# A Mamba-style scan kernel: norm and output stages reordered, both directions summed on TensorE, scan states in SBUF

## The reference

```
x = x + conv(layernorm_over_channels(x))       # conv: norm over the 64x64 pixels, weight, bias,
                                               # dt = softplus(xn . dt_w + dt_b),
                                               # out[t] = exp(dt*A) * out[t-1] + xn[t], t over 1024 channels
t = tokens(x)                                  # 4096 tokens x 1024
xz = (layernorm(t) @ in_proj_w.T).T            # 2 x 2048 channels x 4096 tokens
x, z = split(xz)
y  = direction(x) + reverse(direction(reverse(x)))    # forward and backward weights differ
out = t + nan_to_num((y * silu(z)) @ out_proj_w.T)

direction(x):  xc = conv1d(x) + b ; [dt, B, C] = xc @ xproj_w.T
               u = clip(xc); delta = softplus(clip(dt @ dtproj_w.T + b) + b)
               h[n] = exp(delta * A[n]) * h[n] + (delta * u) * B[n]     # 16 states n, over tokens
               y = sum over n of C[n] * h[n]  +  u * D
```

## Time and profile before

| what | us |
|---|---|
| median of 3 runs | 8618.31 (8612.55 to 8621.57) |
| the profiled execution | 8615.87 |
| its span, first to last instruction | 8614.1 |
| TensorE busy | 7207.2 (84%) |
| VectorE busy | 7548.3 (88%) |
| ScalarE busy | 4928.4 (57%) |
| GpSimd busy | 6814.0 (79%) |

### The profile page before, as it was taken

How to read it: one execution, slowest core, us unless ns; L and a number is a source line. 1 busy time by engine, 2 the same in 40 slices (tenths; PEclk the granted TensorE clock), 3 DMA queues, 4 the chain that set the end, 5 groups by cost and what they waited for, 6 DMA issues and landing times. The chain is left out here.

```text
span 8614.1 us, 107712 instructions
## 1 busy us (share of the span) xinstructions
PE 7207.2 (84%) x28624; PEld 4128.4 (48%) x28624; DVE 7548.3 (88%) x8364; ACT 4928.4 (57%) x11720; POOL 6814.0 (79%) x3026
## 2 busy tenths in 40 slices
PE   7449888888888888876788888888888887769999
PEld 4243455455545555544455545455555555534444
DVE  7940999999999999999999999999999999934443
ACT  2552666666666666666666666666666666610000
POOL 1310999999999999999999999999999999921110
PEclk9679999999999999987899999999999998879999
DMA  3263231313131313121223232323232322154442
GB/s 83 58 188 129 73 112 64 113 65 114 64 113 67 113 64 113 66 100 42 98 73 124 74 126 72 124 76 124 72 124 78 122 73 104 47 175 137 137 138 81
DMA packets 540787, 843.35 MB, mean 98 GB/s; under 512 B 112576, under 2 KB 260032, under 8 KB 522816
## 3 DMA queue, kind: packets, MB, share of 16 engines
q1 hardware_dynamic: 540224, 837.03, 29.4%
HBM read 583.83 MB, written 253.02 MB: 97 GB/s over the span
## 5 line engine op out<-in xcount | busy, mean ns | idle before, releaser
L1114 POOL TENSOR_TENSOR scan_w<-scan_du,scan_bcast_b 128x2048 f32<-128x2048 f32 x1023 | 4629.4, 4537 | 3.6 <-DMA scan_bcast_b<-bc 3.6
L1163 DVE TENSOR_TENSOR_SCAN scan_h<-scan_da,scan_state,scan_w 128x512 f32<-128x512 f32 x3072 | 3787.0, 1282 | 21.8 <-issue 14.5
L920 PE MATMUL scan_yT<-all_ident,scan_hc 128*128 128x128 f32 x12288 | 1992.4, 300 | 1010.9 <-DVE scan_hc L1173 995.5
L1020 ACT ACTIVATE scan_da<-scan_delta,scan_prm 128x512 f32<-128x512 f32 x4096 | 2803.6, 685 | 0.0
L920 PEld LDWEIGHTS scan_yT<-all_ident,scan_hc 128*128 128x128 f32 x12288 | 1466.6, 151 | 1974.6 <-DVE scan_hc L1173 1741.8
L1173 DVE TENSOR_TENSOR scan_hc<-scan_h,scan_bcast_c 128x512 f32<-128x512 f32 x3072 | 1955.5, 682 | 16.9 <-ACT scan_state L1000 16.9
L812 PE MATMUL scan_in_ps<-scan_hn,scan_win 128*128 128x512 f32 x3840 | 1741.0, 596 | 13.3 <-issue 13.3
L1000 ACT ACTIVATE scan_state<-scan_h 128x1 f32<-128x1 f32 x3072 | 518.6, 169 | 1770.7 <-DVE scan_h L1163 1768.8
L1123 POOL TENSOR_TENSOR scan_hp<-scan_hs,scan_bcast_c 128x512 f32<-128x512 f32 x1024 | 1306.5, 1276 | 73.7 <-issue 47.0
L1163 DVE TENSOR_TENSOR_SCAN scan_hs<-scan_da,scan_state,scan_w 128x512 f32<-128x512 f32 x1024 | 1297.5, 1267 | 32.1 <-ACT scan_da L1020 31.9
L812 PEld LDWEIGHTS scan_in_ps<-scan_hn,scan_win 128*128 128x128 f32 x3840 | 697.0, 192 | 723.2 <-issue 723.2
(11 more groups left out here) (128 smaller groups left out, 5547.8 us busy)
## 6 DMA issues: line engine op xcount, KB each, us to landing
yT<-scan_y_out SPq DMA_DIRECT2D x257, 256.0 KB, 2.0
scan_win<-winx SPq DMA_DIRECT2D x128, 512.0 KB, 3.5
xc<-scan_xc_out SPq DMA_DIRECT2D x256, 256.0 KB, 2.0
scan_xc<-xc SPq DMA_DIRECT2D x256, 256.0 KB, 3.6
scan_bcast_b<-bc SPq DMA_DIRECT2D x64, 1024.0 KB, 7.8
scan_bcast_c<-bc SPq DMA_DIRECT2D x64, 1024.0 KB, 7.8
scan_win<-winz SPq DMA_DIRECT2D x128, 512.0 KB, 4.6
scan_x<-x_pad SPq DMA_DIRECT2D x128, 257.5 KB, 2.6
```

The costliest lines, as they stand in the source:

```text
L920: last = nc.tensor.matmul(yT[:, tb], hc[:, i % NOUT, tb * P:(tb + 1) * P], ident[:], is_transpose=True, start=(i == 0 and tb == 0), stop=( ...
L1020: nc.scalar.activation(da[:, n % 2], delta[:, s], ACT.Exp, scale=decay(b, n)).then_inc(S["exp_done"], 1)
L1114: nc.gpsimd.tensor_tensor(w[:, g], du[:, s].unsqueeze(1).to_broadcast([P, G, T]), bcast_b[:, g * G:(g + 1) * G], ALU.mult).then_inc(S["w_d ...
L1163: nc.vector.tensor_tensor_scan(flip(b, h_slot(n)), flip(b, da[:, n % 2]), flip(b, w[:, n // G, n % G]), state_of(b, n), ALU.mult, ALU.add) ...
```

## The change

- Norm (n3): `affine` moves to ScalarE, `add_log` to GpSimd, where it alternates with the scalings, two tiles ahead. ScalarE loads one table set at the start.
- Scan: h moves from PSUM to SBUF. The two banks are y_ps and early_ps. TensorE's new `sum_y(b)`, for forward units, transposes the unit's y_out and the stored y of the backward unit of the same tokens and channels (loaded to y_back by SP) into y_ps: 8 transposes. ScalarE's `y_copy` moves it to y_sum, and SP stores it in y by channels. Only the backward units' sums go to yT now. z_out has one slot instead of two. The zero matmuls around a projection go: its first and last matmul open and close it. TensorE's loop over `before_scan` is written out.
- Out: y and z are loaded, in four slots; no sum on GpSimd, no transposes; VectorE multiplies y and silu(z), both in SBUF. wout is loaded after the first chunk's y and z, and each projection waits for its own tile.

The core of the diff:

```
 stage_channel_scan
+            def scale(j):
+                for s in range(2):
+                    nc.gpsimd.tensor_tensor(xn[...], xn[...], rstd2[:], ALU.mult).then_inc(scaled, 1)
+            def add_log(j):                                     # GpSimd
+                for s in range(2):
+                    pool.wait_ge(relu_done, j * 2 + s + 1)
+                    pool.wait_ge(log_done, j * 2 + s + 1)
+                    nc.gpsimd.tensor_tensor(sp_[:, s], sp_[:, s], mag[:, s], ALU.add).then_inc(sp_done, 1)
+            scale(0)
+            scale(1)
+            with pool.Fori(0, NT // 2 - 2) as j:
+                add_log(j)
+                scale(j + 2)
...
-            def affine(j):                                      # VectorE, tensor_scalar
+            def affine(j):                                      # ScalarE
+                for s in range(2):
+                    act.wait_ge(scaled, j * 2 + s + 1)
+                    nc.scalar.activation(xn[...], xn[...], ACT.Identity, bias=lnb[...], scale=lnw[...]
+                                         ).then_inc(normed, 1)
+            relu(0)                                             # VectorE
+            with dve.Fori(0, NT // 2 - 1) as i:
+                relu(i + 1)
+                scan(i)
+            scan(NT // 2 - 1)
 stage_scan
-        h = sc.ps("h", [P, 2, T])
+        h = sc.sb("h", [P, 2, T])
+        y_ps, early_ps = sc.ps("y_ps", [P, T]), sc.ps("early_ps", [P, T])
-        z_out = sc.sb("z_out", [P, 2, T])
-        zero = sc.sb("zero", [P, T])
+        z_out = sc.sb("z_out", [P, T])
+        y_back, y_sum = sc.sb("y_back", [P, TB, P]), sc.sb("y_sum", [P, T])
...
+            def load_y_back(b):                                 # SP, forward units
+                i = (2 * NCH - 1 - b // DB) * DB + b % DB
+                sp.dma_start(y_back[:], yT_d[i + 1]).then_inc(S["y_loaded"], LOAD)
+            def store_y(b):
+                hold(sp, S["y_copied"], b - HALF + 1, S["passed"])
+                sp.dma_start(y_d[...], y_sum[:]).then_inc(S["stored"], LOAD)
+                if b > HALF:
+                    store_y(b - 1)
+                if b >= HALF:
+                    load_y_back(b)
...
+            def sum_y(b):                                       # TensorE, at step 7 of unit b + 1
+                pe.wait_ge(S["yT_copied"], b + 2)
+                pe.wait_ge(S["y_copied"], b - HALF)
+                for tb in range(TB):
+                    nc.tensor.matmul(y_ps[...], y_out[:, b % 2, tb], ident[:], is_transpose=True,
+                                     start=(tb == 0), stop=False)
+                pe.wait_ge(S["y_loaded"], (b - HALF + 1) * LOAD)
+                for tb in range(TB):
+                    last = nc.tensor.matmul(y_ps[...], y_back[:, tb], ident[:], is_transpose=True,
+                                            start=False, stop=(tb == TB - 1))
+                last.then_inc(S["y_mm"], 1)
...
+            def y_copy(b):                                      # ScalarE, at step 12 of unit b + 1
+                act.wait_ge(S["y_mm"], b - HALF + 1)
+                if b > HALF:
+                    act.wait_ge(S["stored"], stored_to(b))
+                nc.scalar.activation(y_sum[:], y_ps[:], ACT.Copy).then_inc(S["y_copied"], 1)
 stage_out
-        yf, yb = sc.sb("yf", [P, 2, T]), sc.sb("yb", [P, 2, T])
+        NY = 4
+        y = sc.sb("y", [P, NY, T])
...
-                    nc.gpsimd.tensor_tensor(yf[:, s], yf[:, s], yb[:, s], ALU.add).then_inc(summed, 1)
...
-                    nc.vector.tensor_tensor(yg[:, g, u], yt_ps[:, s], sz[:, s], ALU.mult).then_inc(gated, 1)
+                    nc.vector.tensor_tensor(yg[:, g, u], y[:, slot(q, s)], sz[:, slot(q, s)], ALU.mult
+                                            ).then_inc(gated, 1)
...
+                if isinstance(c, int) and c == 0 and q == KT - 1:
+                    for i in range(KT):
+                        sp.dma_start(wout[:, i], wout_d[i]).then_inc(w_loaded[i], LOAD)
```

More of the change, by code:

```diff
@@ L324, in relu @@
                                             ALU.max).then_inc(relu_done, 1)
[L326 to L330, removed]
             def scan(j):
@@ L353, in scan @@
                     nc.vector.tensor_copy(mv[:, ds(j * 4 + s * 2, 2)], mv_t[:, s]).then_inc(chain, 1)
[L355 to L368, removed]
+            relu(0)
+            with dve.Fori(0, NT // 2 - 1) as i:
+                relu(i + 1)
+                scan(i)
             scan(NT // 2 - 1)
@@ L372, in _, with step @@
         def _(act):
[L373 to L380, removed]
+            def affine(j):
+                for s in range(2):
+                    act.wait_ge(scaled, j * 2 + s + 1)
+                    nc.scalar.activation(xn[:, ds(j * (2 * C) + s * C, C)], xn[:, ds(j * (2 * C) + s * C, C)],
+                                         ACT.Identity, bias=lnb[:, ds(j * 2 + s, 1)],
+                                         scale=lnw[:, ds(j * 2 + s, 1)]).then_inc(normed, 1)
+            def step(j, after=True):
                 for s in range(2):
@@ L390, in _ @@
                     nc.scalar.activation(mag[:, s], mag[:, s], ACT.Ln, bias=1.0).then_inc(log_done, 1)
+                if after:
+                    affine(j + 1)
                 for s in range(2):
-                    act.wait_ge(par_loaded, 5 * LOAD)
                     act.wait_ge(sp_done, j * 2 + s + 1)
@@ L396, in _ @@
                                          scale=aneg[:, ds(j * 2 + s, 1)]).then_inc(decay_done, 1)
+            nc.scalar.preload_act_table_set("natural_log_exp_and_others")
+            act.wait_ge(par_loaded, 5 * LOAD)
+            affine(0)
+            nc.scalar.activation(aneg[:], aneg[:], ACT.Exp).then_inc(achain, 1)
+            act.wait_ge(achain, 1)
+            nc.scalar.mul(aneg[:], aneg[:], -1.0).then_inc(achain, 1)
+            act.wait_ge(achain, 2)
+            act.sem_inc(decay_done, 2)
+            act.sem_inc(scan_done, 2)
+            with act.Fori(0, NT // 2 - 1) as j:
+                step(j)
+            step(NT // 2 - 1, after=False)
         @block.tensor
@@ L908, in unit @@
                             project_step(a)
+                    if n == SUM and b > HALF:
+                        sum_y(b - 1)
                     if n == SKIP:
@@ L928, in _ @@
             pe.wait_ge(S["setup"], 3)
-            open_projection()
-            with pe.Fori(0, DB // 2) as j:
+            for j in range(DB // 2):
                 before_scan(j)
-            close_projection()
             dt_matmul(0)
@@ L935, in _ @@
                 unit(b)
+            sum_y(NU - 1)
         @block.scalar
@@ L965, in in_copy @@
                 act.wait_ge(S["in_mm"], i + 1)
-                out = x[:, i % 2, 0:T] if back(i) else z_out[:, i % 2]
+                out = x[:, i % 2, 0:T] if back(i) else z_out[:]
                 nc.scalar.activation(out, in_ps[:], ACT.Copy).then_inc(S["in_copied"], 1)
@@ L1045, in unit @@
                         delta_step(b + 1)
+                    if n == 12 and b > HALF:
+                        y_copy(b - 1)
                     if n == 10:
@@ L1083, in _ @@
             yT_copy(NU - 1)
+            y_copy(NU - 1)
         @block.gpsimd
@@ L1142, in _ @@
             pool.sem_inc(S["hp_done"], NP)
-            nc.gpsimd.memset(zero[:], 0.0).then_inc(S["setup"], 1)
             nc.gpsimd.memset(state[:], 0.0).then_inc(S["setup"], 1)
@@ L1292, in _ @@
         def _(pe):
[L1293 to L1301 removed]
             def project(c, g, q):
+                pe.wait_ge(w_loaded[q], LOAD)
                 if q == 0:
[L1305 to L1306 removed]
+                    pe.wait_ge(gated, c * DB + DB + NY)
                 pe.wait_ge(o_read, c * KT + q + 1)
@@ L1362, in metaformer @@
     bc = scratch("bc", (NCH, 2 * NS, T))
-    yT = [scratch(f"yT{d}", (NCH * DB + 1, P, TB, P)) for d in range(2)]
+    yT, y = scratch("yT", (NCH * DB + 1, P, TB, P)), scratch("y", (DI, HW))
     with Scope(nc, "all") as top:
@@ L1377, in metaformer @@
             stage_token_norm(nc, xn, ident, mv, hnT, x1T, x_pad)
-        stage_scan(nc, ident, hnT, winx, winz, wx, wdt, convp, par, skip, x_pad, xc, z, bc, yT)
-        stage_out(nc, passed, ident, yT[0], yT[1], z, wout, x1T, out)
+        stage_scan(nc, ident, hnT, winx, winz, wx, wdt, convp, par, skip, x_pad, xc, z, bc, yT, y)
+        stage_out(nc, passed, y, z, wout, x1T, out)
 def kernel(**inputs):
```

123 lines of the change are left out of this document (51 added, 72 removed).

## The result

The changed kernel takes 11,562.75 us (median of 4 runs, 11,559 to 11,570), the kernel before 8615.43 in the same comparison: a ratio of 1.342, 95% interval 1.340 to 1.344. The forecast was 11,660, with a range of 10,500 to 12,400.

The account below looks back on a forecast made before the run. VectorE and GpSimd, both full in the scan stage, were taken as the bound: 8614 + 3226 (moving h) - 18 (low-clock excess covered) - 45 (n3) - 117 (out) = 11,660 us, range 10,500 to 12,400.

Parts of the forecast that it names:

- Moving h: Scan stage: multiplications by C with two SBUF inputs take turns with GpSimd, 12.6 us more a unit, 3226 us.
- the 0.6 us for turns that no longer overlap: Scan stage, each unit: 12 x 0.05 us added to the 12.0 us of waits.
- PSUM or SBUF as such: VectorE's instructions: SBUF instead of PSUM saves nothing by the rows; the 62 cycles would save some 200 us.
- sum_y and y_copy: Scan stage, 128 forward units: 1.3 us each on TensorE, hidden; without the cover of longer units 170 us.
- TensorE's clock: Rival, scan stage: at clock 0.5 TensorE becomes the bound, 13,150 us; hidden at 0.74. 8 in 100 for above 12,400.
- n3: Norm stage: VectorE loses affine and add_log, scans may wait for GpSimd; -45 us, between -85 and +15.
- the wait of the scans: n3: each of 32 scans may wait a turn behind GpSimd, at most 59 us more; L336 stays long.
- Out: Out stage: first matmul after 40 us instead of 80, projections without transposes or sum waits; -117 us together.
- no collision: Rival, scan stage: the multiplication stays at 0.59 us, so the kernel gets faster, 8434 us; 3 in 100.
- pairs share one wait: Rival, scan stage: a pair of multiplications pays one wait, 9520 us, or 10,600 with half; 13 in 100 for below 10,500.
- theory A: Memset run's forecast, scan stage: only GpSimd instructions reading SBUF take turns; multiplications behind hp wait 1.0 us; 30.4 us a unit, 9,550 us.

Follow-up runs that it names:

- e2_h_psum: The changed kernel with h back in PSUM and y_ps sharing the bank of in_ps: 8417.22 us, ratio 0.9774 to the kernel before.
- e1_h_sbuf: The kernel before with one edit, h in SBUF (its two banks serve before_scan alone): 11,755.95 us, ratio 1.365.

## Why the prediction was right, point by point

- **Moving h**: right in mechanism, place and size. Forecast 12.6 us a unit; the unit shown has 38.24 us against 25.98, and the stage grew by 3141 us where 3208 (3226 - 18) was forecast. The missing 67 us are 0.3 us a unit. The term that was mis-sized is the 0.6 us for turns that no longer overlap: the unit shown is 25.98 + 12.2 of waits + 0.06. The rule of the Trainium skill (SBUF — State Buffer, Who interferes with whom), which spoke against the change, agrees with the trace in who waits for whom. Taken to the letter, a wait for the whole of the other's instruction, it would have put another 540 us on a forecast that was already 97 us too high.
- **PSUM or SBUF as such**: nothing, as the rows of before had it. In the kernel with one PSUM operand the multiplication takes 675 ns. In the changed kernel the last pair of a unit, which doesn't wait, takes 658 and 677 ns (medians). In the out stage, where GpSimd is idle, the product from PSUM took 684 ns before and the one from two SBUF tiles takes 685. The Trainium skill (VectorE: DVE Perf Modes, the section on the TRN2 errata) gives an instruction that reads PSUM 62 cycles more than one that reads SBUF. They don't show in this instruction.
- **sum_y and y_copy**: hidden, also without the cover of a slow VectorE. I priced that case at 170 us; in e2_h_psum it is 0, since TensorE is busy 265 of the 300 us from 4300 to 4600 there, 23.0 us in a unit of 25.98.
- **TensorE's clock** (a rival): the granted clock was 0.79 with TensorE busy 140 of 200 us, as in the case that I took (0.74). The work stayed hidden: over the stage it is 6949 us, 27.1 a unit of 38.5, at 0.77. The 30 us at 0.74 and the 44.4 at 0.5 of the prediction are too high, since the 22.2 us that they divide were themselves measured at 0.92.
- **n3**: -60 for -45, and the nearness is in part luck. The term that was wrong is the wait of the scans: I gave them 59 us, and said that L336 would stay long to the end. They have no wait (2271 ns). GpSimd's additions wait for ScalarE's Ln, and in the rhythm that results GpSimd is idle while VectorE scans. In exchange the copies of the statistics wait, 33 us, which I had not seen although L353 took 1063 ns in the contended third of before. Of the 251 us VectorE is busy 226; in 20 it waits for TensorE's row sums.
- **Out**: -129 for -117. First matmul 34 us after the stage's start for 40, the projections 882 us for 881 + 5.
- **The rivals**: no collision (3 in 100) is excluded by the changed kernel and e1_h_sbuf, 1699 ns each. That pairs share one wait is excluded by the second multiplications: in pairs two to five nearly all wait as forecast. In the first pair the second one waits in 138 of 256 units only; in the others the next multiplication waits longer, as told below.

## What to carry to other kernels

Before a tile is moved from PSUM to SBUF, count the SBUF inputs of the VectorE instructions that read it. If one of them gets two and GpSimd reads SBUF most of the time, it waits for GpSimd's instruction under way (here seven or eight of twelve did), and the trace shows this as a longer instruction, not as idle time. Whether it waits depends on what GpSimd does at that moment: the scans of n3 have two SBUF inputs and did not wait in the changed kernel (2271 ns), but did before, in the first third (4406 ns in the earlier trace rows). What a wait costs is set by the length of GpSimd's instruction: cutting 2048 columns into four times 512 gave back 1453 of 3141 us although GpSimd had more to do; one operand in PSUM gave back all. The version worth keeping is e2_h_psum: the rest of the change with h in PSUM, 2.3% faster than the kernel before.

## What I had not expected of the hardware

Who gets the turn when both ask at nearly the same time is not settled by the recorded starts. In two neighbouring units of the changed kernel hp (GpSimd's product for one of its four states) starts 0.22 us after the first multiplication. In one the second multiplication waits for hp (pair of 4696.12, 2.33 us); in the other hp waits for both. Timelines of VectorE and GpSimd:

```profile
4657.72 1.26 DVE L1207 TENSOR_TENSOR scan_hc<-scan_h,scan_bcast_c 128x512 f32<-128x512 f32 x2
...
4662.45 2.71 DVE L1207 TENSOR_TENSOR scan_hc<-scan_h,scan_bcast_c 128x512 f32<-128x512 f32 x1
```

```profile
4657.94 2.19 POOL L1158 TENSOR_TENSOR scan_hp<-scan_hs,scan_bcast_c 128x512 f32<-128x512 f32 x1 [1.47 <-issue]
```

The unit loses nothing by it, since the next multiplication then takes 2.71 instead of 1.49 us. hp loses in this way in 118 of the 256 units. In the kernel with memsets it is hp that waits in most units, at all four places, and that is the 4 us a unit by which theory A was too high. GpSimd seems to ask some tenths of a microsecond after its recorded start; why the same distance goes one way here and the other way there stays open.

A VectorE copy of two columns from SBUF to SBUF, 169 ns alone, took 1188 ns in the mean beside GpSimd's scalings: one SBUF input is enough there, unlike in a multiplication.
